# Two layers in rounds of 256 tokens: scores by 64 keys, hidden units made a round ahead, loads in three parts

## What is computed

```python
L = jnp.where(tri, jnp.exp(cs[..., :, None] - cs[..., None, :]), 0.0)
scores = jnp.einsum('znid,znjd->znij', Cc, Bc) * L
y_diag = jnp.einsum('znij,znjh->znih', scores, Xc)
decay_states = jnp.exp(cs[..., -1:] - cs)
states = jnp.einsum('znj,znjd,znjh->zndh', decay_states, Bc, Xc)
```

## Time and profile before

| | us |
|---|---|
| median of 3 timed runs | 734.0 |
| lowest, highest | 732.73, 736.51 |
| the profiled execution | 735.66 |
| its span, first to last instruction | 733.9 |
| TensorE busy | 711.3 (97%) |
| VectorE busy | 497.5 (68%) |
| ScalarE busy | 342.0 (47%) |
| GpSimd busy | 77.2 (11%) |

### The profile page before, as it was taken

One profiled execution on the slowest core, in us unless ns is written; L12 is line 12 of the kernel. 1 busy time (PEld: TensorE's weight loads), 2 busy tenths in 40 slices (PEclk: granted clock), 3 DMA queues, 4 the chain that ended last, 5 costly groups with the idle time before them and its releaser, 6 DMA issues.

```text
span 733.9 us, 17949 instructions
## 1 busy us (share of the span) xinstructions
PE 711.3 (97%) x6896; PEld 590.1 (80%) x6896; DVE 497.5 (68%) x1207; ACT 342.0 (47%) x678; POOL 77.2 (11%) x85
## 2 busy tenths in 40 slices
PE   5998999999999999999999999999999999999998
PEld 3777688877888688886888868888788878888686
DVE  4976599547895478955787558855689547895133
ACT  1411685226832468215762168522584236821690
POOL 6301011101011010100111001110101101011020
PEclk9989999999999999999999999999999999999999
DMA  7900351125400353013531145102540136301360
GB/s 238 404 23 29 102 88 32 15 73 144 75 2 15 88 146 59 2 28 104 117 59 16 30 138 95 32 15 69 142 80 3 15 87 145 59 2 26 119 116 16
DMA packets 122444, 55.93 MB, mean 76 GB/s; under 512 B 104384, under 2 KB 114176, under 8 KB 120832
## 3 DMA queue, kind: packets, MB, share of 16 engines
q1 hardware_dynamic: 122368, 54.76, 30.3%
HBM read 42.35 MB, written 12.40 MB: 75 GB/s over the span
## 4 chain that ended last, share of the span: by engine, by line
PE 76%; DVE 12%; issue 5%; DMA 2%; SPq 2%; ACT 2%; POOL 1%; DVEq 0%; ACTq 0%; POOLq 0%
PE psum L1486 58%; PE psum L1707 2%; PE psum L1722 2%; PE psum L1514 2%; PE psum L1565 1%; PE psum L1760 1%; PE psum L1931 1%; PE psum L1595 1%; PE psum L1733 1%; DVE beats L1085 1%; PE psum L1577 1%; DVE own L992 1%; PE psum L1554 1%; PE psum L1873 1%; SPq L453 1%
## 5 line engine op out<-in xcount | busy, mean ns | idle before, releaser
L602 ACT ACTIVATE BC<-psum 64x256 f32<-64x256 f32 x128 | 81.4, 636 | 3.0 <-PE psum L1486 1.3
L1486 PE MATMUL psum<-xn1T,sb_n_gate 128*128 128x256 f32 x256 | 61.3, 382 | 0.0
L1486 PE MATMUL psum<-xn1T,sb_n_up 128*128 128x256 f32 x256 | 60.6, 380 | 0.4 <-DVE cs_row L1294 0.4
L1486 PE MATMUL psum<-xnT,sb_f_gate 128*128 128x256 f32 x240 | 58.5, 386 | 0.0
L1486 PE MATMUL psum<-xnT,sb_f_up 128*128 128x256 f32 x240 | 57.6, 382 | 0.0
L733 ACT ACTIVATE thFB<-psum 128x512 f32<-128x512 f32 x8 | 4.8, 597 | 104.9 <-PE psum L1486 104.9
L1486 PEld LDWEIGHTS psum<-xn1T,sb_n_up 128*128 128x128 f32 x256 | 48.0, 190 | 6.9 <-DVE cs_row L1294 0.8
L1486 PEld LDWEIGHTS psum<-xn1T,sb_n_gate 128*128 128x128 f32 x256 | 48.0, 190 | 6.8
L1486 PEld LDWEIGHTS psum<-xnT,sb_f_up 128*128 128x128 f32 x240 | 44.8, 190 | 6.4 <-issue 0.3
L1486 PEld LDWEIGHTS psum<-xnT,sb_f_gate 128*128 128x128 f32 x240 | 44.2, 189 | 6.8 <-issue 0.2
L1486 PE MATMUL psum<-sb_f_down,hid 128*128 128x256 f32 x224 | 49.5, 379 | 0.0
(11 more groups left out here) (257 smaller groups left out, 1459.0 us busy)
## 6 DMA issues: line engine op xcount, KB each, us to landing
cs_row<-cs_dram SPq DMA_DIRECT2D x8, 1024.0 KB, 4.9
x_dram<-gate SPq DMA_DIRECT2D x8, 512.0 KB, 2.8
cs_half<-cs_dram SPq DMA_DIRECT2D x16, 256.0 KB, 5.9
hidB<-x_dram SPq DMA_DIRECT2D x8, 512.0 KB, 5.9
b_dram<-B_turned SPq DMA_DIRECT2D x32, 128.0 KB, 3.3
hidB<-b_dram SPq DMA_DIRECT2D x8, 512.0 KB, 4.2
X<-in_x SPq DMA_DIRECT2D x9, 256.0 KB, 3.5
XT<-in_x_turned SPq DMA_DIRECT2D x8, 256.0 KB, 3.6
```

Source lines behind the costliest of these rows:

```text
L602: ins = a_.activation(cols[:, par, 2 * pair:2 * pair + 2, :], src[64 * par:64 * par + 64, :, s, :], ACT.Identity)
L1486: ins = t_.matmul(ps(t, name)[first_row:first_row + rows, col:col + n], w, x, start=(k == 0), stop=(k == len(ws) - 1))
```

## The change

- Scores: a chunk's 128 keys are taken as two halves of 64. The first half is multiplied with all 128 queries, the second with the last 64 only. In every odd chunk the halves of the keys lie in swapped partitions, so X's rows, B's rows and cs_pos are loaded in three transfers (`KEY_ROWS`), and the mask on `cs_row` becomes three instructions, which in rounds with `a` wait until four levels are made.
- VectorE: the last two levels are made ahead of end_args (behind a new wait on the store of the round before), the three compares of the first half of the hidden units run together behind decay_sums, hidden_p 1 right behind hidden_p 0.
- TensorE: the pair p1 is made at the end of the round before (from round 0 on), its two silus on ACT with it; res0 goes ahead of gate_in. In round 0 parts of down_0 go between keys_turned, chunk_states and outputs, and the fillers change: 128 columns instead of 256, p2u 1 to 4, yT 1 to 9, xT1's 6 are replaced by the pair p1. At the start 22 small products run ahead of the first transposes. The final round has B0 ahead of carries, two decayed scores ahead of B_decayed and states_1 ahead of the last hidden_n.

Left out in the diff are the changed counts of semaphores (16 to 48 per load in three parts), the fillings of round 0, and the split of differences into itself and rank_inputs, which round 0 calls behind normed_1; for p0 and p1 `whole` is now true but in round 0.

```diff
@@ -51,14 +51,16 @@
...
-FILLS = [["mix_w", "dw", "w0", "k", "mix_g0", "L0", "M0", "k0T", "p3g", "F0"],
-         ["p0g", "mix_k", "w1", "p1g", "mix_g1", "L1", "M1", "kv", "p3u", "yT"],
-         ["p0u", "mix_r", "p1u", "r", "D0", "g", "p2g", "Y0", "s0"],
+FILLS = [["mix_w", "dw", "w0", "mix_g0", "L0", "M0", "k0T", "p3g", "F0"],
+         ["p0g", "mix_k", "w1", "mix_g1", "L1", "M1", "kv", "p3u", "yT"],
+         ["p0u", "mix_r", "k", "r", "D0", "g", "p2g", "Y0", "s0"],
...
-         ["csum", "C1", "sc0", "st", "n0u", "n2u", "F1"],
+         ["csum", "C1", "sc0", "st", "n0u", "n2u", "F1", "p1u"],
...
-         ["X1", "C0", "sc2", "ys0", "n1g", "n3g"]]
+         ["X1", "C0", "sc2", "ys0", "n1g", "n3g", "p1g"]]
+KEY_ROWS = [(slice(0, P), 0, slice(0, P)), (slice(0, 64), 1, slice(64, P)), (slice(64, P), 1, slice(0, 64))]
...
@@ -425,26 +430,30 @@
...
-                    wait(X_rows, b.count(16, 16))
+                    wait(X_rows, b.count(48, 16))
...
-                    wait(cs_loaded, b.count(48, 16))
+                    wait(cs_loaded, b.count(80, 16))
...
-                    sp_.dma_start(cs_pos[:, :], cs_dram.rearrange("(c p) -> p c", p=P),
-                                  allow_slow_non_contiguous=True).then_inc(cs_loaded, 16)
+                    pos = cs_dram.rearrange("(c two p) -> p c two", two=2, p=P)
+                    by_two = cs_pos[:, :].rearrange("p (c two) -> p c two", two=2)
+                    for to, r, from_ in KEY_ROWS:
+                        sp_.dma_start(by_two[to, :, r], pos[from_, :, r], allow_slow_non_contiguous=True).then_inc(cs_loaded, 16)
...
-                    sp_.dma_start(Xrow.rearrange("p q c d -> p (q c) d"),
-                                  x_dram.rearrange("(c p d) -> p c d", p=P, d=SD)).then_inc(X_rows, 16)
-                    wait(B_rows, b.count(16, 16))
+                    keys = x_dram.rearrange("(c two p d) -> p c two d", two=2, p=P, d=SD)
+                    for to, r, from_ in KEY_ROWS:
+                        sp_.dma_start(Xrow.rearrange("p q (c two) d -> p (q c) two d", two=2)[to, :, r, :],
+                                      keys[from_, :, r, :]).then_inc(X_rows, 16)
+                    wait(B_rows, b.count(48, 16))
...
@@ -550,8 +561,18 @@
...
                     pool.sem_inc(passed, 1)
-                    g.affine_select(out=cs_row[:, :, :], in_=cs_row[:, :, :], compare_op=ALU.is_ge, fill=NEG, base=0,
-                                    pattern=[[0, NQ * SCH], [1, P]], channel_multiplier=-1).then_inc(cs_masked, 1)
+                    if a:
+                        pool.wait_ge(lev_ready, a.count(6, 4))
+                        pool.sem_inc(passed, 1)
+                    by_two = cs_row[:, :, :].rearrange("p (c two) q -> p c two q", two=2)
+                    for last, r, two, base in ((P, slice(0, P), 0, 0), (P, slice(0, P), 1, 64), (64, slice(0, 64), 1, -64)):
+                        m = by_two[r, :, two, :]
+                        ins = g.affine_select(out=m, in_=m, compare_op=ALU.is_ge, fill=NEG, base=base,
+                                              pattern=[[0, NQ * SCH // 2], [1, P]], channel_multiplier=-1)
+                        if last == P:
+                            did(ins)
+                    ins.then_inc(cs_masked, 1)
                 if b:
...
@@ -732,13 +753,16 @@
...
+                def next_gates():
+                    for n in range(2):
+                        ffn_tanh(a.next(), f"p{n}", th[n], None)
+                    exp_tables()
...
-                    ffn_tanh(a, "p0", th[0], th_ready)
-                    exp_tables()
@@ -747,11 +771,10 @@
...
-                    ffn_tanh(a, "p1", th[1], th_ready)
+                    ffn_abs(a, 1)
...
-                    ffn_abs(a, 1)
@@ -780,6 +803,8 @@
...
+                    if a.reg is not None:
+                        next_gates()
...
@@ -1122,6 +1148,8 @@
...
+            def rank_inputs(t):
...
@@ -1332,6 +1360,7 @@
...
+                    hidden_p(a, 1)
@@ -1343,10 +1372,9 @@
...
-                    hidden_p(a, 1)
+                    compare(0)
...
-                    sparse_compare(a, 0, 0)
@@ -1355,19 +1383,20 @@
...
-                    end_args()
...
+                    dve.wait_ge(out_stored, b.count(16, 16))
+                    dve.sem_inc(passed, 1)
...
+                    end_args()
...
-                    sparse_compare(a, 0, 1)
-                    sparse_compare(a, 0, 2)
@@ -1395,6 +1424,7 @@
...
+                    rank_inputs(a.next())
...
@@ -1452,17 +1483,20 @@
...
+                    decayed_scores(0)
+                    decayed_scores(1)
...
-                    for n in (0, 2, 1, 3):
-                        decayed_scores(n)
+                    decayed_scores(2)
+                    decayed_scores(3)
...
+                    states_1()
...
-                    states_1()
...
+            rank_inputs(Tile(None, 0, first=True))
@@ -1699,13 +1733,17 @@
...
                     open_bank(t, name)
+                    pe.sem_inc(passed, 1)
                 ins = [None] * NQ
...
                     c = part * 4 + i
-                    for s in range(NQ):
-                        r = half_rows(s)
-                        ins[s] = t_.matmul(ps(t, names[s])[:, i * P:(i + 1) * P], Bf[r, c * P:(c + 1) * P],
-                                           Cf[r, c * P:(c + 1) * P], start=True, stop=True)
+                    for first in range(2):
+                        k, at = slice(c * P + 64 * first, c * P + 64 * first + 64), 64 * (first ^ (c % 2))
+                        for s in range(NQ):
+                            r = half_rows(s)
+                            ins[s] = t_.matmul(ps(t, names[s])[at:at + 64, i * P + 64 * first:(i + 1) * P], Bf[r, k],
+                                               Cf[r, c * P + 64 * first:(c + 1) * P], start=True, stop=True)
                 for s in range(NQ):
@@ -1900,7 +1938,7 @@
...
-                        t_.matmul(ps(a, name)[:, 0:C], ident[:, :], W["f_gate"][:, 0:C], start=True, stop=True)
+                        t_.matmul(ps(a, name)[:, 0:P], ident[:, :], W["f_gate"][:, 0:P], start=True, stop=True)
...
@@ -1962,8 +2000,6 @@
...
-                    project_p(a, 1, "u")
-                    project_p(a, 1, "g")
@@ -1973,8 +2009,8 @@
...
+                    ssd_proj(b, "res0", "w_res", 0)
...
-                    ssd_proj(b, "res0", "w_res", 0)
@@ -2003,6 +2039,7 @@
...
+                        ffn_p(a.next(), 1)
@@ -2023,7 +2060,7 @@
...
-                    kept_at_work("p2u", 1)
+                    kept_at_work("p2u", 4)
@@ -2039,15 +2076,17 @@
...
-                    keys_turned()
-                    chunk_states()
...
-                    down_part(a, 0, 0, 4)
+                    down_part(a, 0, 0, 2)
+                    keys_turned()
+                    down_part(a, 0, 2, 4)
+                    chunk_states()
+                    down_part(a, 1, 0, 2)
...
-                    down_part(a, 1, 0, 4)
-                    kept_at_work("yT", 1)
+                    down_part(a, 1, 2, 4)
+                    kept_at_work("yT", 9)
@@ -2056,7 +2095,7 @@
...
-                    kept_at_work("xT1", 6)
+                    ffn_p(a.next(), 1)
@@ -2067,10 +2106,11 @@
...
+                    ssd_proj(b, "B0", "w_B", 0)
...
-                    for name, w in (("B", "w_B"), ("C", "w_C")):
-                        for half in range(2):
-                            ssd_proj(b, f"{name}{half}", w, half)
+                    ssd_proj(b, "B1", "w_B", 1)
+                    for half in range(2):
+                        ssd_proj(b, f"C{half}", "w_C", half)
@@ -2092,6 +2132,9 @@
...
+            for _ in range(22):
+                t_.matmul(ps(Tile(None, 0, first=True), "xT")[:, 0:HD], ident[:, :], ident[:, 0:HD], start=True, stop=True)
```

30 lines of the change are left out of this document (18 added, 12 removed).

## The result

The changed kernel takes 736.93 us (median of 20 executions, 735.7 to 738.34), the kernel before in the same comparison 734.59 (20 executions, 731.14 to 737.89): a ratio of 1.0032, with an interval of 1.0021 to 1.0043. It is slower by 2.3 us where 14 less were forecast, and lies outside the forecast's range. The profiled span is 734.8 us against 733.9.

The account below looks back on a forecast made before the run. TensorE, busy 711.3 of 733.9 us, was taken to bound rounds 2 to 6, chains over several engines the start and end. Terms -3.0 - 3.5 - 0.7 - 1.7 - 3.4 - 0.3 - 0.9 - 0.7 took 735.66 to 721.5 us, range 717.5 to 727.

Parts of the forecast that it names:

- its own signs of being wrong: Forecast wrong if a steady round stays at 87.3, within or states wait for VectorE, or four records still take 2.08 us.
- Start: Before the first rank product: 22 small products fill TensorE's wait and bring full speed by 9 us, -1.7 us.
- The clock at 34.5: Round 0, 34.50 to 41.30 us: more filler ahead leaves less idle time, the half-speed clock goes, -3.4 us, bound 0.
- Rival 1: Round 0: the clock falls as before, total 724.9 us; chance 0.17.
- Scores: Scores of each tile: 64 quarter-array records take 1.56 us instead of 1.99, -3.0 us for seven tiles.
- Rivals 2 and 3: Scores: 2, short product waits for long, 724.9 us, chance 0.10; 3, only two quarters run at a time, 732.4, chance 0.03.
- Levels, masks, gate: Around gate_in and high_levels, seven rounds: half of gate_in's 1.5 us wait gained, -0.7 us, bounds +1.5 and -1.5.
- Rival 4: High_levels and within: VectorE's chain shows where cover went, 0.5 us in each of seven rounds, total 725.0; chance 0.10.
- The pair p1: Second pair of hidden units, moved a round earlier: round 7 loses it, -3.5 us; rounds 1 to 6 unchanged.
- Final round: Final round: waits for prefix and decayed scores go, scores shorten, extra loads cost 1.2 us; -0.7 us, bounds +0.6 and -1.5.
- Rival 5: B's three loads land one after another, each further one costing up to 4.19 us; total up to 748.7; chance 0.04.

## Why the prediction was wrong, point by point

Two of its own signs of being wrong came: a steady round takes 88.3 us and not less than 87.3, and the four f_gate records still take 2.07. Round 1 starts at 73.2 and not at 67, and high_levels wait where no wait was forecast. The points in turn:

- **Start, -1.7 forecast, +4.7 measured.** The failed step is "44 records of 0.11 us (a quarter of 0.43 to 0.47 for 256 columns)". A record with 128 weight columns does not cost by its 64 moving columns; it takes 0.215 us, as the weight loads do that lie beside it (45 of them are busy for all of the 9.45 us of the start), and as the records of 128 columns behind it do (0.21). The price per column was taken from products of 256 columns, which start 0.43 us apart there, twice the 0.215 of the loads. The bounds "0 and -2.0" had no loss in them. The second step, a full clock at 9 us, failed as well: neither 20 nor 44 records brought it.
- **The clock at 34.5, -3.4.** The mean clock of 34.50 to 41.30 is 1.00, and the rest of round 0 is 4.0 us shorter against 3.7. That is right against the profiled execution, from which the sum was made. No run shows the 3.4 us by themselves: they are the author's estimate, half of the 6.8 us at a granted clock of 0.50. Most executions have a shorter fall or none; what the runs showed is 2.3 us between the medians of the executions with a fall and without. The prediction said that no row tells whether they have it, and took the dearest case. The reason given (less idle time ahead of it) fits the profiles but wasn't tried apart. Rival 1 falls: no execution of the changed kernel has the fall.
- **Scores, -3.0.** 1.50 to 1.56 us in seven of eight tiles (1.69 in one) against 1.56 forecast. Rivals 2 and 3 fall: a short product doesn't wait here for the long one beside it. If it did, the scores would take as long with 64 columns in half of the records as with 128 in all, and they take 1.50 and 1.91 us.
- **Levels, masks, gate, -0.7 with bounds of 1.5 to both sides; some +6.5 measured.** The gate's wait went, 1.5 us. But high_levels wait 8.0 us in seven rounds. The failed step is "0.4 us is the slack": it was taken from the end of a copy to the start of the product behind it, and that distance is still there when TensorE does wait. There was no slack, and so every tenth by which TensorE came sooner or VectorE later became a wait: 0.4 and 0.79 us. The second is GpSimd's: "may slow by some tenths" was 0.76 us, and on level_next 4, where the text looked only at own_taken and B_by_block. "Neutral for low_taken" held for end_args, which had been ahead of low_taken before as well; putting it behind, as the experiment did, takes 0.45 us off this wait, but the wait at keys_turned came in its place. Rival 4 named this place with 0.5 us; it was 1.1.
- **Not in the sum at all: the gap ahead of p3g**, 0.40 to 0.68 us in rounds 3 to 6 (and 0.33 at the head of round 3). No part of the change is meant to make it; it comes with the place of the instructions. In the kernel before no such gap was seen in a steady round, and 16 idle instructions were enough to end one of 3 us.
- **The pair p1, -3.5 in round 7.** Up to the first product of first_levels round 7 is 3.57 us shorter, so the -3.5 hold. The whole round is 2.4 shorter, as 1.05 us ahead of high_levels and two gaps of 0.2 come behind. Round 0 took the pair in for nothing, as said, and round 1 lost its waits for ACT (0.9).
- **Final round, -0.7 forecast, -1.7 measured.** prefix and n3u no longer wait; the three parts of B's load did not put the 1.2 us on the chain that was set aside for them. Rival 5 falls: neither within nor states have a wait for a load in any round.

With the start mended (10 products) and VectorE's, GpSimd's and ACT's order mended, the kernel takes 724.12 us, 2.6 above the 721.5 of the forecast. The nearness is in part luck: the start gave 0.1 of its 1.7 us, and the places of end_args, of the third mask and of the silus are no part of the change that was forecast. What the runs bear out are the terms for TensorE's own work, the scores and the pair; the two that failed were priced from a row of another kind and from a distance that was no slack.

## What to carry to other kernels

The time from the last producer's end to the consumer's start is slack only as far as it is longer than the same distance where the consumer is known to wait: compare it with a row in which it does wait (here 0.39 us in both kernels). Price a filler product from records of its own shape (here 0.215 us with 64 columns, where a quarter of the 256-column record gave 0.11), and let it end before the data is due. When a program of long unrolled loops changes by a few instructions anywhere ahead, look in the steady rounds for gaps without a releaser before crediting or blaming the change, and shift the program by a few idle instructions to see them move (here 16 of them took away gaps of 3.0 to 3.3 us).

## What the runs showed of the hardware

- A shift of TensorE's program by 16 idle instructions changed the time from 760.4 to 737.4 us. Gaps of 0.3 to 3.3 us came and went with the number of instructions ahead of the loop, at the loop's head, ahead of w_dt or behind the 64 short records of the scores, and 43 of them ended 2.2 to 3.1 us behind the start of a 16 KB packet of the queue of kind `instruction`. That TensorE waits for it is not shown directly.
- TensorE's granted clock was 0.50 over 377 to 382 us, behind 1.48 and 0.64 us of idle time among short products, and 0.50 for 3.4 us behind four of five gaps of 3.0 to 3.3 us, where four records took 2.07 us in place of 1.03. Behind the first of the five it stayed 1.00.
- TensorE started 0.30 to 0.48 us behind the end of the VectorE copies that it waited for ahead of high_levels in the changed kernel (0.39 in four of seven rounds), and 0.05 to 0.15 us behind the end in most other waits for VectorE.
- VectorE's multiplication of 128 x 256 took 1.14 and 1.31 us beside GpSimd's masks and 0.38 to 0.43 elsewhere.
- 64 records of the scores on quarters of TensorE took 1.91 us with 128 columns in all and 1.50 with 64 columns in half of them.
- At the start products ran at half speed until 13.5 us with 10 small products in the changed kernel, 14.0 in the kernel before, 15.5 with none in the changed kernel and 18.3 with 22, though the granted clock of the profile is 1.00 there. What decides it stays open.
- An increment of a semaphore ahead of TensorE's first product takes 0.11 to 0.14 us (16 of them 1.8 us, 48 of them 6.7).
